# Expert tiles of a mixture-of-experts stage: six whole weight chunks or five and a half per tile, and slot rows added in place or stored plainly

## What is computed

```python
topk_vals, topk_idx = jax.lax.top_k(softmax(x @ Wg.T), 2)
topk_vals = topk_vals / sum(topk_vals)
for e in range(8):
    h = silu(x @ w1[e].T) * (x @ w3[e].T)            # 256 -> 704
    out = out + combine[:, e:e + 1] * (h @ w2[e].T)  # 704 -> 256
```

## Time and profile before

| | |
|---|---|
| median of three runs | 799.56 us |
| the profiled execution, device time | 800.65 us |
| its span in the trace | 798.9 us |
| TensorE busy | 739.2 us (93%) |
| VectorE busy | 563.1 us (70%) |
| ScalarE busy | 409.6 us (51%) |
| GpSimd busy | 243.5 us (30%) |
| mean granted TensorE clock | 0.907 of full |
| weight tiles: DMAs, size, median to landing | 15 of 2304 KB, 15.5 us |

### The profile page before, as it was taken

One profiled execution on the slowest core, in us unless ns is written; L12 is line 12 of the kernel. 1 busy time (PEld: TensorE's weight loads), 2 busy tenths in 40 slices (PEclk: granted clock), 3 DMA queues, 4 the chain that ended last, 5 costly groups with the idle time before them and its releaser, 6 DMA issues.

```text
span 798.9 us, 15708 instructions
## 1 busy us (share of the span) xinstructions
PE 739.2 (93%) x5988; PEld 589.1 (74%) x5988; DVE 563.1 (70%) x874; ACT 409.6 (51%) x891; POOL 243.5 (30%) x282
## 2 busy tenths in 40 slices
PE   8889998899999989979989799998889998999998
PEld 6633333678888767867876598986678877899997
DVE  5998997578887856777968665655668846555552
ACT  2878888234544434534444666664245541445442
POOL 2032112413432234432457022232124313133231
PEclk8955555799999999999989999999989999999999
DMA  6099999102211113311111011112001035999962
GB/s 193 26 154 170 173 170 180 55 14 87 75 53 61 48 35 91 92 53 34 53 46 60 7 40 34 48 47 66 27 28 54 28 133 186 379 390 391 353 185 67
DMA packets 110456, 87.65 MB, mean 110 GB/s; under 512 B 71281, under 2 KB 92017, under 8 KB 110386
## 3 DMA queue, kind: packets, MB, share of 16 engines
q1 hardware_dynamic: 107842, 83.16, 36.9%
q0 software_dynamic: 2544, 3.54, 2.2%
HBM read 66.49 MB, written 3.41 MB: 88 GB/s over the span
## 4 chain that ended last, share of the span: by engine, by line
PE 57%; DVE 17%; issue 9%; ACT 7%; DMA 6%; POOL 3%; SPq 1%; DVEq 1%; POOLq 0%; ACTq 0%
PE ps L200 10%; PE ps L2423 10%; PE ps L202 9%; PE ps L201 9%; PE ps L1715 4%; PE ps L2098 2%; DVE x L1482 2%; PE ps L1695 2%; DVE qrot L2270 2%; PE ps L1185 2%; ACT kres L960 2%; DMA ptj<-kres 2%; POOL nb L867 1%; DMA tw<-w_l1f 1%; ACT soft L2231 1%
## 5 line engine op out<-in xcount | busy, mean ns | idle before, releaser
L332 POOL TENSOR_TENSOR wa_lo<-raw,wa_hi 128x256 fp32r<-128x256 f32 (+1 forms) x76 | 85.6, 1130 | 189.5 <-ACT wa_hi L321 189.1
L332 POOL TENSOR_TENSOR wb_lo<-raw,wb_hi 128x256 fp32r<-128x256 f32 (+1 forms) x68 | 61.5, 909 | 129.2 <-ACT wb_hi L321 129.2
L2423 PE MATMUL ps<-xgt,tw 128*128 128x128 f32 x720 | 84.5, 278 | 1.5 <-DMA tw<-w_l1f 1.5
L960 ACT ACTIVATE kres<-ps,nb,qs 128x1024 int16<-128x1024 f32 x64 | 76.9, 1202 | 17.1 <-POOL nb L867 11.7
L2423 PEld LDWEIGHTS ps<-xgt,tw 128*128 128x128 f32 x720 | 83.3, 195 | 1.7 <-issue 1.7
L1089 DVE TENSOR_REDUCE nm<-ps 128x1 f32<-128x1024 f32 x64 | 77.4, 1222 | 7.7 <-PE ps L796 6.1
L796 PE MATMUL ps<-qkt 48*128 48x512 bf16 x128 | 65.4, 616 | 5.7 <-ACT kres L960 5.0
L200 PE MATMUL ps<-xt_hi,wa_hi 128*128 128x512 f32 (+1 forms) x168 | 69.1, 411 | 1.3 <-DVE soft L1340 0.9
L201 PE MATMUL ps<-xt_lo,wa_hi 128*128 128x512 f32 (+1 forms) x168 | 65.3, 389 | 0.0
L202 PE MATMUL ps<-xt_hi,wa_lo 128*128 128x512 f32 (+1 forms) x168 | 65.1, 388 | 0.0
L200 PE MATMUL ps<-wb_hi,ot_hi 128*128 128x256 f32 x192 | 57.2, 298 | 1.5 <-DVE ot_lo L2275 0.9
(11 more groups left out here) (428 smaller groups left out, 1906.6 us busy)
## 6 DMA issues: line engine op xcount, KB each, us to landing
tw<-w_l1f SPq DMA_DIRECT2D x15, 2304.0 KB, 15.5
raw<-w_l0a SPq DMA_DIRECT2D x16, 256.0 KB, 2.9
raw<-w_l1p SPq DMA_DIRECT2D x32, 128.0 KB, 2.1
raw<-w_l1x SPq DMA_DIRECT2D x32, 128.0 KB, 2.1
raw<-w_l1a SPq DMA_DIRECT2D x16, 256.0 KB, 2.6
raw<-w_l0f SPq DMA_DIRECT2D x12, 256.0 KB, 2.7
raw<-w_l0a SPq DMA_DIRECT2D x16, 128.0 KB, 2.1
wv_raw<-w_l0a SPq DMA_DIRECT2D x8, 256.0 KB, 3.1
```

Of the source, the lines that this page charges most:

```text
L332: last = nc.gpsimd.tensor_tensor(split_lo, src, split_hi.bitcast(F32), ALU.subtract)
L960: nc.scalar.activation(ei[:, n % RING, :], slot(n), ACT.Exp, bias=nb[:, n % 3:n % 3 + 1], scale=qs[:, col:col + 1], accum_out=sums[:, u, k ...
L2423: last = nc.tensor.matmul(up_gate(m, g)[:, k * P:(k + 1) * P], tw[:, slot_of_tile(m), k, (2 * g + c) * P:(2 * g + c + 1) * P], xgt[:, u, c ...
```

## The change

What it does, part by part:

- **Weights of a tile.** Five whole chunks and one half: `load_tile` now issues five DMAs. One brings the gate and up columns of five chunks (640 rows of 2048 bytes), two the gate and the up weights of the 64 own units of the shared chunk (256 rows of 256 bytes each), laid side by side as one block of 64 + 64 units; one brings the down columns of five chunks (640 rows of 1024 bytes), one the down rows of the shared chunk (128 rows of 1024 bytes). The first three count on `tile_loaded`, the last two on `down_loaded`, which only `down_high` and `down_last` wait for.
- **Products.** `up` has 20 matmuls for five chunks and 2 for the half block, whose output has gate in partitions 0 to 63 and up in 64 to 127 (`up_half`). Silu and the product each become one operation on 640 columns and one on 64 x 128; the masks and their three operations go. The second half of the last chunk of `hx` is set to zero once, and `down` keeps its 18 matmuls.
- **Slot rows.** A token's first pair has the row of the token, its second the row 512 further (`token1`); unused slots have rows of their own (`spare_row`). `rows_d` has 3072 rows of 1 KB and is filled with zeros by one DMA behind tile 0's load. The scatter is a plain store with no wait for the one before; `scaled` waits for the store two back. `xn_d` holds xn twice, with four stores in place of two, so that a gather finds it under either row. `x` isn't copied to DRAM any more.
- **The end.** SP loads the two kinds of rows in two halves each (four DMAs of 256 KB), GpSimd adds the kinds (two operations of 128x512), VectorE adds their sum to x (two more operations) and then the placed rows. `last_places` takes two more small operations.
- **Elsewhere.** One more iota on GpSimd and two fewer small VectorE operations in the dispatch tables, a memset of 128x256 on GpSimd at the start of the stage before, and a wait of SP for the zeros ahead of the loads of tiles 1 to 14.

The diff, cut to its core:

```diff
+            by_row = w_l1f.rearrange("k p m -> (k p) m")
+
+            def load_tile(r, slot, first, half, row):
+                chunks = w_l1f[bass.ds(first, FULL)].rearrange("k p m -> p k m")
+                sp.dma_start(tw[:, slot, 0:FULL, 0:4 * P], chunks[:, :, 0:4 * P]).then_inc(tile_loaded[r], 16)
+                for g in range(2):
+                    units = w_l1f[bass.ds(half, 1), :, 2 * P * g:2 * P * (g + 1)].rearrange("a p (c m) -> (a p) c m", c=C2)[:, :, bass.ds(row, P // 2)]
+                    sp.dma_start(tw[:, slot, FULL, 0:2 * P].rearrange("p (c g m) -> p g c m", c=C2, g=2)[:, g], units).then_inc(tile_loaded[r], 16)
+                sp.dma_start(tw[:, slot, 0:FULL, 4 * P:6 * P], chunks[:, :, 4 * P:6 * P]).then_inc(down_loaded[r], 16)
...
+                sp.dma_start(tw[:, slot, FULL, 4 * P:6 * P], by_row[bass.ds(at, P), 4 * P:6 * P]).then_inc(down_loaded[r], 16)
...
-            sp.wait_ge(x_ready, 10)
-            sp.dma_start(sums_d[0:NTOK].rearrange("(t p) d -> p t d", p=P), x[:]).then_inc(sums_set, 16)
...
+            sp.wait_ge(mo["zeros"], mo_at("zeros", 1))
+            sp.dma_start(rows_d[:].rearrange("(t p) d -> p t d", p=P), zeros.unsqueeze(1).broadcast_to([P, 2 * NT + SLOTS, D])).then_inc(rows_set, 16)
+            for a in range(2):
+                for k in range(2):
...
+            sp.wait_ge(rows_set, WV + 16)
             sp.wait_ge(mo["expert"], mo_at("expert", 1))
...
-            sp.wait_ge(added, 16 * PLACED)
-            sp.dma_start(x[:], sums_d[0:NTOK].rearrange("(t p) d -> p t d", p=P)).then_inc(xn_stored, 16)
+            for r in range(2):
+                sp.wait_ge(rows_out[r], 16 * ((PLACED + 1 - r) // 2))
+            for k in range(2):
+                for a in range(2):
+                    first = a * NTOK + k * 2 * P
+                    sp.dma_start(rows_x[a][:, k * 2 * D:(k + 1) * 2 * D].rearrange("p (t d) -> p t d", d=D), rows_d[first:first + 2 * P].rearrange("(t p) d -> p t d", p=P)).then_inc((xn_stored, rows_set)[k], 16)
...
                 for g in range(2):
-                    for k in range(CHUNKS):
+                    for k in range(FULL):
...
+                for c in range(C2):
+                    last = nc.tensor.matmul(up_half(m), tw[:, slot_of_tile(m), FULL, c * P:(c + 1) * P], xgt[:, u, c, :], start=c == 0, stop=c == 1)
...
-                if m:
-                    pool.wait_ge(added, 16 * m)
-                else:
-                    pool.wait_ge(sums_set, WV + 32)
-                nc.gpsimd.indirect_dma_start(sums_d[:, :], bass.IndirectOffsetOnAxis(scatter_idx[:, m:m + 1], 0), og[:, m % 2, :], None, compute_op=ALU.add).then_inc(added, 16)
+                if m == 0:
+                    pool.wait_ge(rows_set, WV + 16)
+                nc.gpsimd.indirect_dma_start(rows_d[:, :], bass.IndirectOffsetOnAxis(scatter_idx[:, m:m + 1], 0), og[:, m % 2, :], None).then_inc(rows_out[m % 2], 16)
...
+            for k in range(2):
+                cols = slice(k * 2 * D, (k + 1) * 2 * D)
+                pool.wait_ge((xn_stored, rows_set)[k], WV + (96, 48)[k])
+                nc.gpsimd.tensor_tensor(rows_x[0][:, cols], rows_x[0][:, cols], rows_x[1][:, cols], ALU.add).then_inc(mo["both"], 1)
...
-                ends = slice(0, P), slice(WIDE - P, WIDE)
-                for k in range(2):
-                    nc.scalar.activation(act_g[:, m % 2, ends[k]], up_gate(m, 0)[:, ends[k]], ACT.Silu, scale=masks[:, k, m:m + 1])
-                nc.scalar.activation(act_g[:, m % 2, P:WIDE - P], up_gate(m, 0)[:, P:WIDE - P], ACT.Silu).then_inc(mo["gate"], 1)
+                nc.scalar.activation(act_g[:, m % 2, 0:FULL * P], up_gate(m, 0), ACT.Silu)
+                nc.scalar.activation(*half, ACT.Silu).then_inc(mo["gate"], 1)
...
-                act.wait_ge(tile_loaded[r], TURNED + 16 * (m // RAWS + 1))
+                act.wait_ge(down_loaded[r], DOWN_AT + 32 * (m // RAWS + 1))
...
-                nc.vector.tensor_tensor(hx[:], act_g[:, m % 2, :], up_gate(m, 1), ALU.mult).then_inc(mo["h"], 1)
+                nc.vector.tensor_tensor(hx[:, 0:FULL * P], act_g[:, m % 2, 0:FULL * P], up_gate(m, 1), ALU.mult)
+                nc.vector.tensor_tensor(*half, ALU.mult).then_inc(mo["h"], 1)
...
-            dve.wait_ge(xn_stored, WV + 48)
             for k in range(2):
+                dve.wait_ge(mo["both"], mo_at("both", k + 1))
+                nc.vector.tensor_tensor(x[:, 2 * k:2 * k + 2, :], x[:, 2 * k:2 * k + 2, :], rows_x[0][:, k * 2 * D:(k + 1) * 2 * D].rearrange("p (t d) -> p t d", d=D), ALU.add).then_inc(step, 1)
+            for k in range(2):
+                dve.wait_ge(step, c.up())
                 dve.wait_ge(mo["placed"], mo_at("placed", k + 1))
                 nc.vector.tensor_tensor(x[:, 2 * k:2 * k + 2, :], x[:, 2 * k:2 * k + 2, :], last_rows(k), ALU.add).then_inc(mo["total"], 1)
```

116 lines of the change are left out of this document (64 added, 52 removed).

## The result

The changed kernel took 791.12 us (median of 5 runs, 787.31 to 792.43); the kernel before, beside it, 798.89 (796.43 to 800.40). The ratio is 0.9876, with an interval of 0.9837 to 0.9915: faster, as forecast. In terms of the 799.56 us that the forecast started from it is 799.56 x 0.9876 = 789.7 us. The forecast was 791.9, with a range from 790.0: the gain was about two microseconds larger than the sum of my steps, and 0.3 us outside the range. The interval of the ratio, in the same terms, reaches from 786.5 to 792.8 us and holds the forecast too, so this one comparison can't tell the two apart; what went wrong has to be read from the steps. Over all executions in this study the medians are 790.7 (22 executions, 786.7 to 794.6) and 800.0 (129, 794.8 to 806.5), so 9.3 us.

A forecast was written before the change was run, and what follows sets the result against it. The prediction took TensorE's work, busy for 93% of the span, as the bound. Terms - 6.26 - 1.07 - 1.82 + 0.9 + 0.6 = - 7.65 us, from the median 799.56, gave 791.9 us; range 790.0 to 798.5.

The forecast's parts named there:

- TensorE's part: Tile loop: four records fewer per up product save 0.447 us a tile, 6.26 us over fourteen tiles.
- The hole: TensorE's idle before tile 1's up product: weights in time, gather unchanged, 1.07 us gained; clock slightly likelier kept, 1.82 us more.
- rival 1: Before tile 1: the clock falls all the same, 1.82 us stay lost, tile 2 not late; 792.9 us; chance 25%.
- the 0.9 us of new wait for tile 2: Loop start: with the clock kept, TensorE waits 0.9 us for tile 2's up weights.
- The weight stream: Tile weight loads with gather and scatter: 6.97 us a tile, under the loop's 7.22, so hidden after the start.
- rivals 2 and 3: Weight stream paces the loop: part of the gain remains, 796.3 us (20%), or slower than before, 805 us (17%).
- the line through two full streams: DMA row price: 0.010 us a row plus 0.0364 us per 1000 bytes, giving 101 engine-us a tile.
- the single loads: DMA row price from single loads: a tile costs 121 engine-us, against 101 taken.
- Other queues: SP, ScalarE, VectorE, GpSimd: transfers, zeros, xn stores, Silu and the scatter's dropped wait change nothing.
- The end: After the last tile: VectorE's added sums and the rows' loads cost 0.6 us, between 0.4 and 1.6.
- Wrong if something upstream of 670 us moves: Stated sign of failure: the prediction is wrong if anything before 670 us in the trace moves.
- the low end, 790.0: Range's lower limit: a gather 1.1 us earlier and tile 2 in time.

The follow-up runs named there:

- rows_only: Kernel before with only the plain stores and end sums, tiles of six whole chunks with one transfer and masks: 799.88 us, ratio 0.9992.
- after: The changed kernel, first profile and timing, against the kernel before: 791.12 us, ratio 0.9876.
- after_again: The changed kernel run again word for word, against the kernel before: 790.47 us, ratio 0.9878.
- before: The kernel before the change, unchanged, first profile and timing: 798.89 us.
- rows_512: Changed kernel with each tile's 1280 KB transfer cut into four of 512-byte rows: 801.71 us, ratio 1.0012 to the kernel before.
- chain_plain: Changed kernel with each plainly storing scatter again waiting for the one before to land: 791.88 us, ratio 0.9876 to the kernel before.
- half_only: Changed kernel with the half chunk but without plain stores, scatters adding into sums_d one after another: 794.77 us, ratio 0.9940 to the kernel before.
- gather_ahead: Changed kernel with tile 1's down half issued only once tile 1's gather is issued: 788.35 us, ratio 0.9828 to the kernel before.
- after_p4: The changed kernel word for word, for a fourth profile: ratio 0.9858 to the kernel before.

## Why the prediction was right or wrong

**TensorE's part: right, a little short.** The up product is 4.91 us as forecast. The rest of a turn took 7.27 - 4.91 = 2.36 us in place of 7.67 - 5.36 = 2.31, so a tile gained 0.40 and not 0.447: 12 turns gave 4.73 where I had 5.36. The 0.05 us lie among the same down matmuls and transposes. The split of the product into two blocks isn't what adds them, since `rows_only` has it not and takes 7.73 - 5.36 = 2.37 us; what does stays open.

**The hole: wrong, and this is the largest error of the stage.** I kept the gather's landing and gave the whole wait for weights back. The gather landed 9.8 to 10.6 us after `expert_of` in the changed kernel and 9.9 to 10.3 before, and in `after` TensorE idled 1.56 + 0.47 = 2.03 us instead of 1.57. The clock fell in three of four profiles of the changed kernel. So rival 1, and not my forecast, is what usually happens in the stage; its price was also too low, since it had the gather in time. In `after_again`, whose clock was kept as I had assumed, the stage was 121.7 us, a gain of 7.8 against `before` and of 8.2 against the mean of before, where 7.65 was forecast. That is partly luck: the 0.9 us of new wait for tile 2 never came, and the loop gained 0.6 less than forecast.

**The weight stream: right.** 6.9 us a tile against 6.97, and rivals 2 and 3 (37% together) did not come. `rows_512` puts the price of a row at 0.0097 us in a full stream, so the line through two full streams was the right one and the single loads were the wrong end. Tile 2's forecast wait of 0.9 us never came: no profile of the changed kernel shows TensorE waiting for `tw`. The rule of the Trainium skill on rows under 512 bytes ("DMA: Bandwidth & Descriptors", "Specifications") would, by the estimate made from it ahead of the result, have put the stream level with the loop, at 7.26; the stream kept 6.9 with 512 rows of 256 bytes in it. A penalty in that size is not visible here, though the rows weren't tried alone.

**Other queues: one step wrong in its reason.** "The scatter no longer waits for its predecessor ... nothing there either." As a statement about the wait it is true (`chain_plain`). But I had looked for late gathers and not at the chain of scatters itself, which was slower than a turn of the old loop already and had 0.3 to 2.8 us of slack at its end. The new loop takes that slack away, and 2.8 us of the gain of the half chunk would have been lost to it (`half_only`). The forecast came out right because both halves were in the change; a forecast for the half chunk alone, by my steps, would have been about 3 us too good. Zeros, stores and SyncE's issue cost nothing, as forecast: the four xn stores were issued from 656.06 on in 2.25 us and took 2.4 us each, so they were done near 660, six microseconds ahead of the first tile load at 666.63.

**The end: right within 0.2 us.** From tile 14's product on it took 16.1 to 16.4 us in the four profiles of the changed kernel, 16.2 in `after` and `after_again`, against 16.12 - 0.447 + 0.6 = 16.3 forecast.

**Ahead of the stage: the step that put the time outside the range.** The sum has no term for anything ahead of the stage, so it puts that at nothing, and the range gives it no room. In the first pair of profiles it was 4.3 us. The mean stage is 129.9 us before and 123.4 after, a gain of 6.5 where 7.65 was forecast; the whole gained 9.3, so 2.8 us of it lie ahead of the stage over all executions. In the eight profiles of the two kernels the difference there is 2.3 us, and it is a matter of how often the clock fell: 5, 6, 7 and 9 units between 147 and 660 us in the changed kernel, 8, 9, 9 and 9 before. That is two fewer on average, 3.4 clock-us, and nothing is left over in favour of the changed kernel. For the executions without a profile there is only the mean granted clock, by which 1.6 us less were lost in the changed kernel's, about 0.4 of it in the hole. That mean also counts the first 147 us, in which the profiles lost 53 to 58 clock-us while the operation at 145 us moved by only 2.1 us; it can't settle the rest. Whether the changed program by itself makes the clock fall less often, by where it lies in memory for example, or these executions drew fewer falls, was not tried and stays open.

"Wrong if something upstream of 670 us moves" was the right warning, but the range had no room for it: the low end, 790.0, counted only the gather and tile 2. With 2 us for what lies ahead of the stage it would have held 789.7. That the forecast came within 2.2 us is itself luck in part, since the 2.0 us too many in the stage of the first pair and the 4.3 us ahead of it have opposite signs.

## What to carry to other kernels

When a loop gets shorter, look for chains beside it that do not shrink with it, and for the slack that hides them (here the scatters, 92 to 94 us from first to last, with 0.3 to 2.8 us of slack): a part that is worth nothing alone can be what lets another part count. Price a DMA row from two full streams, not from single loads. Where a needed small transfer and a large early one are issued together, issue the small one first: 1.4 us of delay for the large one bought 1.1 us at the start of the loop. And split the trace at an event ahead of the change before comparing, since the part before it moved by up to 6 us between executions of the same kernel.

## What the runs showed of the hardware

- An adding scatter of 128 rows took 7.6 us from issue to landing under a full weight stream (`half_only`) and a storing one 6.5 (`chain_plain`). In series the adding ones started 7.7 to 9.8 us apart under the stream and 4.6 to 5.2 behind it; the storing ones kept pace with a turn of 7.27.
- A gather issued together with 0.64 MB of weights on another queue landed 1.1 us later than one issued 1.5 us ahead of them (`after_again` against `gather_ahead`): in these runs the order of issue carried over between queues.
- The clock before tile 1 fell to its lower level of 1.2 GHz in four profiles with a gather wait of 1.48 to 1.76 us, and stayed at 2.4 GHz where the wait was 0.9, 1.0 and 1.4. With the fall (0.55 granted over 3.6 us) the product of 4.91 us took 6.81.
- Five to ten such falls per profile came ahead of the stage, at changing places even where the program was the same (`after` to `after_p4`: at 403 and 437 us in one, at 278, 363 and 442 in another).
